# Last diagonal step of a group in full fp32 from summed operands, and a first block by two tiles

## The chip, the cores and the metric

The kernel runs on one core of a Trainium2 chip. The metric is the device time of that core in microseconds (us), read for the whole program. The engines are TensorE (PE in the profile, with its weight loads as PEld), VectorE (DVE), ScalarE (ACT), GpSimd (POOL) and SyncE (SP), which issues most of the DMAs.

## What is computed

An attention block and a channel mix on x of shape (2, 2048, 256), each with a layer norm without parameters in front and a residual behind. All matrices are 256x256 and fp32:

```
def attention(y):                       # y = layernorm(x)
    q = (y @ Wq + bq) / sqrt(256); k = y @ Wk + bk; v = y @ Wv + bv
    scores = where(causal, q k^T, -inf)         # 2048 x 2048 per batch
    return (softmax(scores) @ v) @ Wo + bo
def channel_mix(x):                     # x = layernorm(x)
    x_prev = x shifted by one row, first row 0
    xr = mu_r * x + (1 - mu_r) * x_prev;  xk = mu_k * x + (1 - mu_k) * x_prev
    return sigmoid(xr @ W_r.T) * (square(relu(xk @ W_k.T)) @ W_v.T)
x = x + attention(layernorm(x))
x = x + channel_mix(layernorm(x))
```

## The kernel before

**Numbers.** Most matmuls take operands rounded to fp32r. So that the result is near fp32, an operand is kept as a pair: ScalarE copies it out of PSUM as `_hi` in fp32r, VectorE or GpSimd subtracts that and leaves `_lo`. A product is then three matmuls, hi by hi, hi by lo and lo by hi (`product`, lines 794, 797 and 798). With 256 channels there are two chunks of 128 to contract (`KC` = 2), so one product is six matmuls. A few matmuls take plain fp32 operands without a split: the products of the weight matrices (lines 1002 and 1027).

**Tiles.** The 4096 rows are 32 tiles of 128. Four tiles make a group (512 queries), and the last of eight groups is treated in two halves. For each group the normalised rows are transposed (`xT`), multiplied by a folded matrix of Wq and Wk to give the keys (`kT`) and by a folded Wv and Wo to give the values (`v`). Then come steps of scores: step s takes 128 keys and all queries of the group that see them, so transposed scores of 128 x 512. The four steps on the diagonal see 512, 384, 256 and 128 queries. The last of them would have 128 columns. `scores` (lines 909 to 921) widens it to 256, so its six matmuls have 256 columns each, of which 128 are used. The causal mask is added by one bf16 matmul (line 796).

**After the scores.** ScalarE keeps a copy of the scores in a slot of `st` (16 slots of 512 columns), VectorE updates a running maximum (`take_max`), TensorE transposes the maximum (`mt`), VectorE reduces it, TensorE spreads it (`mb`), VectorE subtracts it (`shift`), ScalarE takes the exponential and rounds to `p_hi`, GpSimd makes `p_lo` (`weights_low`, line 364), and TensorE multiplies by the values (`pv`, lines 961 to 963, three matmuls per tile). The channel mix follows per group: transposes `hT`, products `kk`, `rr`, `ff`.

**Order.** Every engine runs one list, written by a loop over slots. In slot s stands score step s while there are any (79 of them), and the tables at lines 114 to 129 say in which slot each other stage stands (`PV_AT`, `XT_AT`, `KT_AT`, `V_AT`, `HT_AT`, `KK_AT`, `STATS_AT`, `APPLY_AT` and so on). All engines read the same tables, so a slot number sets the order on each engine, and semaphores do the rest. PSUM banks of TensorE's stages go round among three (`bank_w`), so a stage also waits until the stage three uses earlier has been read out (`free`).

**The start.** Ahead of the loop TensorE transposes the raw weights (line 969), multiplies Wk by Wq in plain fp32 into one bank (line 1002), transposes the first group (line 830), and makes its keys with twelve matmuls of 512 columns (line 1017). `idle` (line 986) runs matmuls on zeros in between, with counts from `IDLE`. ScalarE and VectorE take hi and lo of the folded matrix in one instruction each. On VectorE `ln1_apply` (line 595) writes the normalised rows, tile by tile, and a memset (line 599) closes a group.

Of the kernel before, what the change touches and what calls it, by code (L numbers as in the profile page):

```python
# [5 lines left out]
def attention_channel_mix_block(nc, y, wq, bq, wk, bk, wv, bv, wo, bo, w_r, w_k, w_v, mu_r, mu_k, out):  # L6
# [10 lines left out]
    B, T, C = y.shape  # L17
# [133 lines left out]
    LEAD = 2  # L151
    SLOTS = range(FIRST_SLOT, END)
# [34 lines left out]
    with ctx:  # L187
# [16 lines left out]
        peak = sb("peak", [P, 2, GW])  # L204
        peak_col = sb("peak_col", [P, 2, TG])
# [40 lines left out]
        early = (bank_o + bank_w[:NO - 1:-1])[:4]  # L246

# [3 lines left out]
        def bank_of(*use):  # L251
# [11 lines left out]
         last_mix_split, last_act_split, squared, single_squared, act_high, act_split, r_ready, gate_ready, ff_ready, ff_used, out_ready, last_out_ready) = [sem(n) for n in (  # L263
# [6 lines left out]
            "last_mix_split last_act_split squared single_squared act_high act_split r_ready gate_ready ff_ready ff_used out_ready last_out_ready").split()]  # L270
# [57 lines left out]
        def _(pool):  # L328
# [760 lines left out]
```

## Time and profile before

| | us |
|---|---|
| median of three runs | 365.44 (364.97 to 365.71) |
| the profiled execution | 365.21 |
| its span, first to last instruction | 363.2 |
| TensorE busy in the span | 353.2 (97%) |
| VectorE busy | 254.8 (70%) |
| ScalarE busy | 239.2 (66%) |
| GpSimd busy | 209.0 (58%) |

The span is what the trace covers; 2.0 us of the profiled execution lie around it. A matmul's record is longer than the distance to the next one, since matmuls are pipelined: what one costs is read from start to start. In a row of the timeline the first number is the start, the second the length of the piece, and xN the number of instructions that it merges.

### The profile page before, as it was taken

The numbers are of one execution on the slowest core, as the hardware profiler recorded it, in microseconds if no ns is written. First come the engines' busy times: TensorE is split into PE (matmuls) and PEld (weight loads), VectorE is DVE, ScalarE is ACT, GpSimd is POOL, SyncE is SP. The second block draws the span as 40 slices with busy tenths as digits, with TensorE's granted clock in tenths as the row PEclk, the third lists the DMA queues.
The fourth block names the chain that finished last, engine by engine and source line by source line (L and its number), as shares of the span: only waits on it lengthen the run. The fifth ranks groups of instructions, "written<-read, shape, count | busy, mean of one in ns | idle before, by whom it ended". The sixth has DMA issues, their size and how long they took to land.

```text
span 363.2 us, 6783 instructions
## 1 busy us (share of the span) xinstructions
PE 353.2 (97%) x2466; PEld 324.5 (89%) x2466; DVE 254.8 (70%) x569; ACT 239.2 (66%) x467; POOL 209.0 (58%) x246
## 2 busy tenths in 40 slices
PE   8999999999999999999999999999999999999995
PEld 6788888989899888899998989999999999989885
DVE  4597888698946786855568876786857558673645
ACT  2355543987659547597565679587368877789572
POOL 4013330468777743579644357678155768699781
PEclk9999999999999999999999999999999999999999
DMA  7600000000012003003000000030000000000001
GB/s 214 220 2 1 2 0 3 0 3 1 2 38 79 1 0 117 1 2 90 28 3 0 2 0 3 29 88 1 3 29 31 0 3 2 30 31 0 31 29 58
DMA packets 11905, 10.64 MB, mean 29 GB/s; under 512 B 1889, under 2 KB 11874, under 8 KB 11874
## 3 DMA queue, kind: packets, MB, share of 16 engines
q1 hardware_dynamic: 10512, 10.23, 8.8%
q8 instruction: 19, 0.31, 0.4%
q10 hardware_dynamic: 1362, 0.01, 0.2%
q14 instruction: 12, 0.10, 0.1%
HBM read 6.04 MB, written 4.19 MB: 28 GB/s over the span
## 4 chain that ended last, share of the span: by engine, by line
PE 76%; DVE 8%; POOL 6%; ACT 5%; issue 3%; DMA 1%; SPq 0%; ACTq 0%; DVEq 0%
PE W L794 16%; PE W L797 16%; PE W L798 15%; PE O L961 7%; PE O L963 7%; PE O L962 7%; PE W L830 3%; POOL kT_hi L364 3%; DVE mix L710 2%; DVE h_row L696 1%; POOL mix_lo L369 1%; DMA h_row<-in_L_attn_Wq_dram 1%; DVE st L675 1%; ACT mix L471 1%; ACT st L416 1%
## 5 line engine op out<-in xcount | busy, mean ns | idle before, releaser
L364 POOL TENSOR_TENSOR p_lo<-st,p_hi 128x512 fp32r<-128x512 f32 (+1 forms) x71 | 80.9, 1157 | 38.8 <-ACT p_hi L416 37.7
L663 DVE TENSOR_TENSOR peak<-peak,W 128x512 f32<-128x512 f32 (+3 forms) x70 | 42.2, 603 | 47.9 <-ACT st L416 47.7
L416 ACT ACTIVATE st<-W 128x512 f32<-128x512 f32 (+1 forms) x79 | 42.5, 538 | 42.3 <-PE W L798 42.2
L961 PE MATMUL O<-v_hi,p_hi 128*128 128x258 f32 x241 | 69.1, 287 | 0.2 <-DVE x_in L685 0.2
L963 PE MATMUL O<-v_hi,p_lo 128*128 128x258 f32 x241 | 68.0, 282 | 0.0
L962 PE MATMUL O<-v_lo,p_hi 128*128 128x256 f32 x241 | 67.7, 281 | 0.0
L797 PE MATMUL W<-xT_lo,kT_hi 128*128 128x512 f32 (+2 forms) x188 | 65.9, 350 | 0.0
L794 PE MATMUL W<-xT_hi,kT_hi 128*128 128x512 f32 (+2 forms) x188 | 64.4, 343 | 0.8 <-DVE kT_lo L573 0.8
L798 PE MATMUL W<-xT_hi,kT_lo 128*128 128x512 f32 (+2 forms) x188 | 63.2, 336 | 0.0
L452 ACT ACTIVATE st<-st 128x512 f32<-128x512 f32 (+1 forms) x79 | 44.8, 567 | 8.7 <-DVE st L675 8.6
L416 ACT ACTIVATE p_hi<-st 128x512 fp32r<-128x512 f32 (+1 forms) x71 | 40.4, 569 | 15.3 <-PE O L963 13.4
L369 POOL TENSOR_TENSOR mix_lo<-mix,mix_hi 128x512 fp32r<-128x512 f32 (+2 forms) x36 | 40.4, 1147 | 17.5 <-ACT mix_hi L416 17.5
L961 PEld LDWEIGHTS O<-v_hi,p_hi 128*128 128x128 f32 x241 | 45.4, 188 | 1.2 <-POOL p_lo L364 0.5
L962 PEld LDWEIGHTS O<-v_lo,p_hi 128*128 128x128 f32 x241 | 45.6, 189 | 0.3
L963 PEld LDWEIGHTS O<-v_hi,p_lo 128*128 128x128 f32 x241 | 45.5, 189 | 0.0
L675 DVE TENSOR_TENSOR st<-st,B 128x512 f32<-128x512 f32 (+1 forms) x79 | 43.2, 609 | 3.1 <-PE B L941 3.1
L794 PEld LDWEIGHTS W<-xT_hi,kT_hi 128*128 128x128 f32 x188 | 35.5, 189 | 3.6 <-DVE kT_lo L573 1.1
L798 PEld LDWEIGHTS W<-xT_hi,kT_lo 128*128 128x128 f32 x188 | 35.6, 190 | 3.3
L794 PE MATMUL W<-ffn_hi,mix_hi 128*128 128x256 f32 x128 | 37.0, 289 | 1.3 <-DVE mix_lo L573 0.7
L797 PEld LDWEIGHTS W<-xT_lo,kT_hi 128*128 128x128 f32 x188 | 35.9, 191 | 2.3
L797 PE MATMUL W<-ffn_lo,mix_hi 128*128 128x256 f32 x128 | 36.2, 282 | 0.0
L798 PE MATMUL W<-ffn_hi,mix_lo 128*128 128x256 f32 x128 | 36.1, 282 | 0.0
(138 smaller groups left out, 824.3 us busy)
## 6 DMA issues: line engine op xcount, KB each, us to landing
out_dram<-gate SPq DMA_DIRECT2D x15, 256.0 KB, 2.1
x_in<-in_L_attn_y_all_dram SPq DMA_DIRECT2D x7, 512.0 KB, 4.5
x_in<-in_L_attn_y_all_dram SPq DMA_DIRECT2D x2, 256.0 KB, 4.8
h_row<-in_L_attn_Wk_dram SPq DMA_DIRECT2D x1, 256.0 KB, 3.1
h_row<-in_L_attn_Wq_dram SPq DMA_DIRECT2D x1, 256.0 KB, 4.3
st<-in_L_attn_Wv_dram SPq DMA_DIRECT2D x1, 256.0 KB, 5.3
st<-in_L_attn_Wo_dram SPq DMA_DIRECT2D x1, 256.0 KB, 5.5
mix<-in_L_ffn_W_k_dram SPq DMA_DIRECT2D x1, 256.0 KB, 6.6
```

The costliest lines, as they stand in the source:

```text
L364: g.tensor_tensor(lo[:, r], score_tile(u), hi[:, r].bitcast(f32), ALU.subtract).then_inc(p_split, 1)
L369: g.tensor_tensor(mix_lo[:, j, r], mix[:, j, r], mix_hi[:, j, r].bitcast(f32), ALU.subtract).then_inc(mix_split, 1)
L416: a.activation(dst, src, ACT.Copy, **kw).then_inc(done, 1)
L452: a.activation(score_tile(u), score_tile(u), ACT.Exp).then_inc(exp_done, 1)
L663: v.tensor_tensor(peak[:, J % 2, r], peak[:, J % 2, r], scores, ALU.max).then_inc(maxed, 1)
L675: v.tensor_tensor(score_tile(u), score_tile(u), bank_b[:, cols_of(u)], ALU.subtract).then_inc(sub_done, 1)
L794: mm(dst, a_hi, b_hi, start=n == 0, stop=False)
L797: mm(dst, a_hi, b_lo, start=False, stop=False)
L798: last = mm(dst, a_lo, b_hi, start=False, stop=end)
L961: mm(o[:, 0:VW], hi[:, r], v_hi[:, j + b, :], start=j + b == 0, stop=False)
L962: mm(o[:, 0:C], hi[:, r], v_lo[:, j + b, :], start=False, stop=False)
L963: last = mm(o[:, 0:VW], lo[:, r], v_hi[:, j + b, :], start=False, stop=end)
```

## The change

Four things change.

1. The last diagonal step of each group of four tiles (seven of them) is no longer widened and split. GpSimd adds `_hi` and `_lo` again, into `own_x` (128 queries, two chunks, in the unused first half of an `st` slot) and `own_k` (128 keys), and TensorE multiplies these as plain fp32 with 128 columns: two matmuls and the mask instead of six and the mask. GpSimd does the two additions (128x256 each) in the slot before that step.
2. The first group is done by two tiles: the product of Wk and Wq goes chunk by chunk into two banks, the first transposes start once two tiles are normalised, and the keys are made with 24 matmuls of 256 columns instead of 12 of 512.
3. The counts of idle matmuls go from (6, 1, 5, 6, 1) to (6, 1, 3, 0, 0).
4. All tables of slots have new numbers.

```diff
-    XT_AT = {1: (2, 2), 2: (7, 9), 3: (23, 23), 4: (33, 34), 5: (43, 43), 6: (47, 50), 7: (61, 61)}
+    XT_AT = {1: (2, 2), 2: (8, 10), 3: (22, 23), 4: (31, 32), 5: (42, 42), 6: (48, 49), 7: (60, 60)}
...
-    FT_AT = [(-2,), (3,), (3,)]
-    IDLE = (6, 1, 5, 6, 1)
+    FT_AT = [(2,), (7,), (10,)]
+    IDLE = (6, 1, 3, 0, 0)
...
+    OWN_AT = [FIRST[J + 1] - 2 for J in range(NJ) if GROUPS[J][2] == TG]
...
+            def own(J):
+
+                G = GROUPS[J][0]
+                if J > 0:
+                    pool.wait_ge(s_ready, FIRST[J])
+                pool.wait_ge(xT_split, KC * (G + 1))
+                pool.wait_ge(kT_split, KC * (G + 1))
+                x, k = slice(GW - P, GW), slice(GW * (G % GB + 1) - P, GW * (G % GB + 1))
+                n = PLACES[FIRST[J + 1] - 2][0]
+                if n >= NR:
+                    pool.wait_ge(p_split, FILLED[n - NR] + 1)
+                g.tensor_tensor(own_x(J), xT_hi[:, G % NT, :, x].bitcast(f32), xT_lo[:, G % NT, :, x].bitcast(f32), ALU.add).then_inc(own_ready, 1)
+                g.tensor_tensor(own_k[:], kT_hi[:, :, k].bitcast(f32), kT_lo[:, :, k].bitcast(f32), ALU.add).then_inc(own_ready, 1)
...
             for s in SLOTS:
                 for u in P_IN[s]:
                     weights_low(u)
+                if s in OWN_AT:
+                    own(STEPS[s][0])
...
-            sc.wait_ge(fold_ready, 3)
-            high(wkq_hi[:], pairs(bank_b), fold_moved, scale=SCALE)
             for h in range(KC):
-                xT_part(0, h)
+                sc.wait_ge(fold_ready, 3 + h)
+                high(wkq_hi[:, h, :], folded[h][:, 0:C], fold_moved, scale=SCALE)
+            for i in range(2):
+                sc.wait_ge(xT_ready, i + 1)
+                high(xT_hi[:, 0, :, i * 2 * P:(i + 1) * 2 * P], pairs(bank_of("xT", 0, i)), xT_high)
...
-                if t == TG - 1:
-                    dve.wait_ge(xhat_done, TG * (G + 1))
-                    v.memset(xhat[:, :, 0:1], 1.0).then_inc(xhat_ready, 1)
+                if t == TG - 1 or G == 0 and t == 1:
+                    dve.wait_ge(xhat_done, TG * G + t + 1)
+                    v.memset(xhat[:, t - 1 if G == 0 else 0:t + 1, 0:1], 1.0).then_inc(xhat_ready, 1)
...
+                if n == TG and diagonal(s) == TG - 1:
+                    pe.wait_ge(own_ready, 2 * (J + 1))
+                    r = cols_of(s)
+                    mm(bank[:, r], own_k[:, 0, :], own_x(J)[:, 0, :], start=True, stop=False)
+                    mm(bank[:, r], ident_b[:], mask_b[:, P:], start=False, stop=False)
+                    mm(bank[:, r], own_k[:, 1, :], own_x(J)[:, 1, :], start=False, stop=True).then_inc(s_ready, 1)
+                    return
...
-            pe.wait_ge(q_taken, 1)
-            for h in range(KC):
-                for d in range(KC):
-                    last = mm(bank_b[:, h * C:(h + 1) * C], wkT[:, d, h * P:(h + 1) * P], wqT[:, d, :], start=d == 0, stop=d == KC - 1)
-            last.then_inc(fold_ready, 1)
+            for d in range(KC):
+                pe.wait_ge(q_taken, d + 1)
+                for h in range(KC):
+                    last = mm(folded[h][:, 0:C], wkT[:, d, h * P:(h + 1) * P], wqT[:, d, :], start=d == 0, stop=d == KC - 1)
+                    if d == KC - 1:
+                        last.then_inc(fold_ready, 1)
```

The instructions of TensorE at the start, from the product of the weight matrices (line 1002) to the first keys (line 1017), before:

```order
L1002 MATMUL B<-st 128x256 x4
L986 MATMUL O<-p_lo 128x512 x6
L830 MATMUL W<-ident,xhat 128x128 x8
L969 MATMUL O<-ident,st 128x128 x4
L986 MATMUL O<-p_lo 128x512
L1017 MATMUL W<-xT_hi,wkq_hi 128x512
```

And the same place now, where L1043 is that product, L866 the transposes of the first group and L1064 the keys:

```order
L1043 MATMUL B<-st 128x256 [waits q_taken,taken_ready,bias_ready]
L1043 MATMUL O<-st 128x256
L1043 MATMUL B<-st 128x256 [waits q_taken]
L1043 MATMUL O<-st 128x256
L866 MATMUL W<-ident,xhat 128x128 [waits xhat_ready]
L866 MATMUL W<-ident,xhat 128x128 x3
L1010 MATMUL O<-ident,st 128x128 [waits wv_loaded]
L1010 MATMUL O<-ident,st 128x128 x3
L866 MATMUL W<-ident,xhat 128x128 [waits xhat_ready]
L866 MATMUL W<-ident,xhat 128x128 x3
L1064 MATMUL W<-xT_hi,wkq_hi 128x256 [waits xT_high,fold_moved]
```

The seven idle matmuls are gone from here, the transposes stand in two halves with the transposes of Wv between them, and the keys start with 256 columns.

GpSimd's list behind the start, before; `rstd` is the factor of the layer norm for the next group:

```order
L394 COPY st<-cols 128x2 [waits col_loaded]
L349 TENSOR_SCALAR var_eps<-mean_var 128x4 [waits var1_ready]
L351 TENSOR_TENSOR rstd<-var_eps,minus_half 128x4 [waits eps1_ready]
L349 TENSOR_SCALAR var_eps<-mean_var 128x4 [waits var1_ready]
L351 TENSOR_TENSOR rstd<-var_eps,minus_half 128x4 [waits eps1_ready]
L364 TENSOR_TENSOR p_lo<-st,p_hi 128x512 [waits p_high]
```

And now:

```order
L417 COPY st<-cols 128x2 [waits col_loaded]
L358 TENSOR_SCALAR var_eps<-mean_var 128x4 [waits var1_ready]
L360 TENSOR_TENSOR rstd<-var_eps,minus_half 128x4 [waits eps1_ready]
L386 TENSOR_TENSOR st<-xT_hi,xT_lo 128x256 [waits kT_split,xT_split]
L387 TENSOR_TENSOR own_k<-kT_hi,kT_lo 128x256
L358 TENSOR_SCALAR var_eps<-mean_var 128x4 [waits var1_ready]
L360 TENSOR_TENSOR rstd<-var_eps,minus_half 128x4 [waits eps1_ready]
L373 TENSOR_TENSOR p_lo<-st,p_hi 128x512 [waits p_high]
```

The first pair of sums stands directly behind the factor of group 1. The other six pairs stand the same way in the slot before the last diagonal step of their group.

TensorE near the end, at the transposes `hT` of the last groups (L830 before), before; rows L961 to L963 are `pv`, rows L794 to L798 behind them the second half of `ff` of group 6:

```order
L963 MATMUL O<-v_hi,kT_hi 128x258
L830 MATMUL W<-ident,h_row 128x128 [waits h_ready,gate_ready]
L830 MATMUL W<-ident,h_row 128x128
L830 MATMUL W<-ident,h_row 128x128 [waits h_ready,gate_ready]
L830 MATMUL W<-ident,h_row 128x128
L830 MATMUL W<-ident,h_row 128x128 [waits h_ready,ff_used]
L794 MATMUL W<-ffn_hi,mix_hi 128x256 [waits act_split,mu_done]
L797 MATMUL W<-ffn_lo,mix_hi 128x256
```

And now, where L858 is the transpose and L1002 to L1004 are `pv`:

```order
L1004 MATMUL O<-v_hi,kT_hi 128x258
L858 MATMUL W<-ident,h_row 128x128 [waits h_ready,gate_ready]
L858 MATMUL W<-ident,h_row 128x128
L858 MATMUL W<-ident,h_row 128x128 [waits h_ready,ff_used]
L858 MATMUL W<-ident,h_row 128x128
L1002 MATMUL O<-v_hi,kT_lo 128x258 [waits p_split]
L1003 MATMUL O<-v_lo,kT_lo 128x256
L1004 MATMUL O<-v_hi,kT_hi 128x258
```

The third transpose, which waits for `ff_used`, no longer follows the other two: thirteen tile products of `pv` (39 matmuls) stand between, and both halves of `ff` stand ahead of all of them.

## Rows read from the trace of the kernel before

**Rows 1.** The page: busy time by engine, and the chain that ended last.
```profile
PE 353.2 (97%) x2466; PEld 324.5 (89%) x2466; DVE 254.8 (70%) x569; ACT 239.2 (66%) x467; POOL 209.0 (58%) x246
...
PE 76%; DVE 8%; POOL 6%; ACT 5%; issue 3%; DMA 1%; SPq 0%; ACTq 0%; DVEq 0%
```

**Rows 2.** Timeline of TensorE, a masked score step with 256 columns, then group 1's transposes.
```profile
23.60 0.28 PE L794 MATMUL W<-xT_hi,kT_hi 128*128 128x256 f32 x1
23.72 0.23 PE L796 MATMUL W<-mask_b,ident_b 128*128 128x128 bf16 x1
23.76 0.36 PE L797 MATMUL W<-xT_lo,kT_hi 128*128 128x256 f32 x1
23.96 0.28 PE L798 MATMUL W<-xT_hi,kT_lo 128*128 128x256 f32 x1
...
24.32 0.28 PE L798 MATMUL W<-xT_hi,kT_lo 128*128 128x256 f32 x1
24.94 1.16 PE L830 MATMUL W<-ident,xhat 128*128 128x128 f32 x8 [0.34 <-DVE xhat L599]
```

**Rows 3.** Timeline of TensorE at the start: plain fp32 product, idle matmuls, transposes.
```profile
1.44 2.93 PE L986 MATMUL O<-p_lo 128*128 128x512 f32 x6 [1.44 <-DVE p_lo L629]
...
7.46 1.97 PE L1002 MATMUL B<-st 128*128 128x256 f32 x8
9.08 1.75 PE L986 MATMUL O<-p_lo 128*128 128x512 f32 x6
10.67 1.03 PE L830 MATMUL W<-ident,xhat 128*128 128x128 f32 x8
11.54 0.60 PE L969 MATMUL O<-ident,st 128*128 128x128 f32 x4
```

**Rows 4.** Timeline of TensorE: first keys, fold of Wv and Wo, first scores.
```profile
12.22 0.40 PE L1017 MATMUL W<-xT_hi,wkq_hi 128*128 128x512 f32 x1
...
14.97 1.03 PE L1027 MATMUL O<-st 128*128 128x256 f32 x4
...
17.52 0.60 PE L979 MATMUL W<-ident,mix 128*128 128x128 f32 x4
17.88 0.48 PE L794 MATMUL W<-xT_hi,kT_hi 128*128 128x512 f32 x1
```

**Rows 5.** Timeline of ScalarE at the start.
```profile
6.48 0.84 ACT L532 ACTIVATE st<-O,minus_first 128x255 f32<-128x255 f32 x2
```

**Rows 6.** Timeline of VectorE at the start, its rows for xhat among them.
```profile
8.60 0.73 DVE L595 TENSOR_SCALAR xhat<-x_in,mean_var,rstd 128x256 f32<-128x256 f32 x2 [0.26 <-POOL rstd L351]
9.62 0.74 DVE L595 TENSOR_SCALAR xhat<-x_in,mean_var,rstd 128x256 f32<-128x256 f32 x2 [0.29 <-POOL rstd L351]
...
18.35 0.69 DVE L573 TENSOR_TENSOR wvo_lo<-O,wvo_hi 128x512 fp32r<-128x512 f32 x1 [1.49 <-ACT wvo_hi L416]
...
22.81 0.56 DVE L663 TENSOR_TENSOR peak<-peak,W 128x384 f32<-128x384 f32 x1 [0.19 <-ACT st L416]
23.28 1.38 DVE L595 TENSOR_SCALAR xhat<-x_in,mean_var,rstd 128x256 f32<-128x256 f32 x4
```

**Rows 7.** Timeline of GpSimd at the start.
```profile
21.86 1.04 POOL L351 TENSOR_TENSOR rstd<-var_eps,minus_half 128x4 f32<-128x4 f32 x1
```

**Rows 8.** Groups of instructions by form: GpSimd's subtractions (line, form, xcount, busy, mean ns).
```profile
L364 POOL TENSOR_TENSOR p_lo<-st,p_hi 128x512 fp32r<-128x512 f32 x50 | 64.7, 1309 | 30.9 <-ACT p_hi L416 29.9
L364 POOL TENSOR_TENSOR p_lo<-st,p_hi 128x256 fp32r<-128x256 f32 x7 | 5.6, 805 | 0.0
```

**Rows 9.** VectorE's instructions on the tile h_row: ns min/median/max.
```profile
L696 DVE TENSOR_SCALAR h_row<-x_in,mean_var,per_tile x32: 406/412/1462, 43.1 to 351.1; 128x256 f32<-128x256 f32 x32
```

**Rows 10.** Timeline of VectorE, then of GpSimd, around 94.3 us.
```profile
94.24 0.76 DVE L696 TENSOR_SCALAR h_row<-x_in,mean_var,per_tile 128x256 f32<-128x256 f32 x1
...
93.56 1.29 POOL L378 TENSOR_TENSOR mix_lo<-mix,mix_hi 128x512 fp32r<-128x512 f32 x1
```

**Rows 11.** Waits of TensorE: what for, us in total, times, longest.
```profile
PE B L932 <- DVE peak L663: 0.9, 1, 0.9
PE W L794 <- DVE kT_lo L573: 0.8, 1, 0.8
PE W L794 <- DVE mix_lo L573: 0.7, 1, 0.7
PE W L830 <- DVE gate L742: 0.7, 1, 0.7
...
PE W L794 <- DVE gate L742: 0.3, 1, 0.3
PE O L961 <- DVE x_in L685: 0.2, 1, 0.2
```

More of the change, by code:

```diff
@@ L131, in stages @@
+    END = 674
+    FT_AT = [(2,), (7,), (10,)]
+    IDLE = (6, 1, 3, 0, 0)
     def stages(s):
@@ L204, in attention_channel_mix_block @@
         peak = sb("peak", [P, 2, GW])
+        own_k = sb("own_k", [P, KC, P])
         peak_col = sb("peak_col", [P, 2, TG])
@@ L246, in attention_channel_mix_block @@
         early = (bank_o + bank_w[:NO - 1:-1])[:4]
+        folded = (bank_b, early[0])
         def o_of(G, p):
@@ L831, in transposes, with first_xT @@
                 return last
+            def first_xT(i):
+                pe.wait_ge(xhat_ready, i + 1)
+                for h in range(KC):
+                    for t in range(2):
+                        last = nc.tensor.transpose(bank_of("xT", 0, i)[:, (2 * h + t) * P:(2 * h + t + 1) * P], xhat[:, 2 * i + t, h * P:(h + 1) * P], ident[:])
+                last.then_inc(xT_ready, 1)
             def xT(G, h):
                 free("xT", G, h)
-                pe.wait_ge(xhat_ready, G + 1)
+                pe.wait_ge(xhat_ready, G + 2)
                 transposes(bank_of("xT", G, h), xhat, h, range(TG)).then_inc(xT_ready, 1)
@@ L1004, in _ @@
             idle(IDLE[3])
-            for h in range(KC):
-                xT(0, h)
+            first_xT(0)
             pe.wait_ge(wv_loaded, 16)
             transposed(raw_v, early[2])
+            first_xT(1)
             idle(IDLE[4])
             xh, xl = xT_hi[:, 0], xT_lo[:, 0]
-            pe.wait_ge(fold_moved, 1)
-            for w, x, done in ((wkq_hi, xh, xT_high), (wkq_lo, xh, fold_split), (wkq_hi, xl, xT_split)):
-                for k in range(KC):
-                    pe.wait_ge(done, 1 if done is fold_split else k + 1)
-                    for h in range(KC):
-                        last = mm(bank_of("kT", 0, h)[:], w[:, k, h * P:(h + 1) * P], x[:, k, :], start=x is xh and w is wkq_hi and k == 0,
-                                  stop=x is xl and k == KC - 1)
-                        if x is xl and k == KC - 1:
-                            last.then_inc(kT_ready, 1)
+            for i in range(2):
+                c = slice(i * 2 * P, (i + 1) * 2 * P)
+                for w, x, done in ((wkq_hi, xh, xT_high), (wkq_lo, xh, fold_split), (wkq_hi, xl, xT_split)):
+                    for k in range(KC):
+                        if done is fold_split:
+                            pe.wait_ge(done, k + 1)
+                        else:
+                            pe.wait_ge(fold_moved, k + 1)
+                            pe.wait_ge(done, i + 1)
+                        for h in range(KC):
+                            last = mm(bank_of("kT", 0, h)[:, c], w[:, k, h * P:(h + 1) * P], x[:, k, c], start=x is xh and w is wkq_hi and k == 0,
+                                      stop=x is xl and k == KC - 1)
+                            if x is xl and i == 1 and k == KC - 1:
+                                last.then_inc(kT_ready, 1)
```

57 lines of the change are left out of this document (29 added, 28 removed).

## The prediction

> **What bounds the kernel now.** I read the page's busy times first, then the chain that ended last, then TensorE's waits, and last its timeline from start to start. TensorE is busy 97% of the span and is 76% of the chain; GpSimd, the engine that gets new work, is busy 58% [rows 1]. TensorE's waits are few and short: the longest behind the start are 0.9, 0.8, 0.7 and 0.7 us, once each [rows 11]. So the kernel is a row of matmuls issued without a break, and a matmul taken out anywhere gives back its own pitch (start to start), unless it stood just ahead of a wait. What the other engines do counts only where it makes one of those waits longer or shorter. The profiled execution took 365.21 us, 2.0 more than its span of 363.2; the median of the runs is 365.44. I sum against 365.21 and add 0.2 at the end.
>
> **Part 1, the last diagonal step.** Before, it is six matmuls of 256 columns and a mask. The step shown has the same form: it starts at 23.60, its last matmul at 24.32, and a pitch is 0.12, so it ends at 24.44 and costs 0.84 us [rows 2]. The mask's share is 0.12: 0.04 to the next start, and 0.20 instead of 0.12 behind that. Now there are two plain fp32 matmuls of 128 columns and the same mask. The trace has no such matmul, but it has two neighbours. A plain fp32 matmul of 256 columns appears as two records: four of them are the 8 records from 7.46 to 9.08, 0.20 us each. A plain fp32 transpose of 128 columns is one record: 8 of them from 10.67 to 11.54, 0.109 each [rows 3]. Lower bound: half the columns, half the time, 0.10 a record. Upper bound: no shrinking at all, 0.20. I take 0.11, from the row that has 128 columns and the same weight load. Four records and the mask: 4 x 0.11 + 0.12 = 0.56. Saved: 0.28 a step, 7 steps, **1.9 us** (2.2 at the lower bound; at the upper 4 x 0.20 + 0.12 = 0.92, a loss of 0.6).
>
> What it adds is on GpSimd: two sums of 128x256 a group, 14 in all. The nearest row is a subtraction of that form, 0.8 us [rows 8]: 1.6 us a group, 11 us over the span, on an engine with 154 us free. It is hidden if the pair is done when TensorE reaches the step. I went through the seven places. Groups 1, 3, 5 and 6 have little on GpSimd there. In group 2 (slot 22) the pair stands behind the `p_lo` of step 10, which waits for an earlier `pv`: after that `pv` come the exponential's copy and `p_lo` (about 1.6 us) and the pair (1.6), against 4.1 us of TensorE work (a score step 0.84, half an `xT` 0.44, half a `v` 1.4, a `pv` 1.4). In group 4 (slot 42) ten `pv` follow, and the next `p_lo` behind the pair cannot start before the first of them is done anyway. So I cost it at nothing there. If that cover went, it would cost up to 1.6 us a group.
>
> **Part 2, the start.** Before: the product at 7.46, first transposes at 10.67, keys at 12.22, fold of Wv and Wo at 14.97 [rows 3, 4]. Now: the two activations that the product waits for run from 6.48 to 7.32 [rows 5], and the product may start on the first, at about 6.95, to end at about 8.7. Two tiles are normalised at 9.33 [rows 6], so the first half of the transposes runs from 9.45 to 9.9, Wv's to 10.35, and the second half waits for tile four at 10.36 and the memset: 10.5 to 10.95. The keys: 24 x 0.118 = 2.85 us from 10.95, to 13.8, if hi and lo keep up. VectorE's lo of the folded matrix stands behind the last tile, at 10.5 to 11.2, its first lo of `xT` at 11.8, and TensorE asks for that one at 11.9. So 13.85 against 14.97: **1.1 us** earlier, and the first scores 1.1 us earlier too, once the transposes of an FFN matrix (0.36, 17.52 to 17.88 [rows 4]), now in slot 2, are set aside.
>
> Then comes the place that decides what remains: group 1's transposes, which already waited for VectorE at 24.94, 0.5 us later than the pitch would have it [rows 2]. VectorE has one instruction fewer ahead (a lo of an FFN matrix), so its statistics end about 1.7 us earlier, and GpSimd's factor, ready at 22.90 before [rows 7], comes at about 21.2. But `xhat` of group 1 also stands behind two running maxima, which follow the scores: 23.28 before [rows 6], about 21.9 now, and four instructions of it take 1.38. Undisturbed it ends at 23.3, TensorE arrives at 22.95, and the wait shrinks to 0.4. It is not undisturbed: GpSimd's first pair of sums stands right behind that factor, from about 21.2 to 22.8. What happens to VectorE then is in the trace. `h_row` is the same kind of instruction as `xhat`, a tensor by scalars from SBUF to SBUF, and takes 0.41 us in the median and up to 1.46 [rows 9]; the one at 94.24 took 0.76, beside a GpSimd subtraction that ran until 94.85 [rows 10]. It stands still until GpSimd's instruction is through. So I expect `xhat` to end at about 24.2 and the transposes to start at 24.3 instead of 24.94. Set against that, 0.36 us of transposes still has to be done behind it. What is left of the 1.1 us is **0.3**. Bounds: 0.2 with all of the pair in the way, 1.25 with none.
>
> The Trainium skill has this as a rule (SBUF — State Buffer, Who interferes with whom): VectorE in its two-port mode and GpSimd take a shared pair of ports for a whole instruction, and the other fully blocks. The trace agrees, as the 1.46 us against 0.41 shows. By a view in which the two engines don't meet, the start would give the 1.25.
>
> **Part 3, idle matmuls.** Nine of 19 go. They filled waits and nothing waits for them: two ahead of the product and six ahead of the transposes stood where TensorE waits for ScalarE and VectorE anyway, as counted above. So they count nothing.
>
> **Part 4, the tables.** They move no work in or out, so they can only change waits. Behind the start the waits of [rows 11] are, at a pitch of 0.12, somewhat dearer from start to start than the view says. (a) The wait for `kT_lo`, 0.8 (0.9 from start to start): the lo of group 3's keys stood on VectorE behind four residual chains; it now stands a slot earlier, ahead of two of them, and two score-sized stages follow before its bank is asked for. Gone. (b) The wait of a transpose for `gate`, 0.7 (0.9): now 39 matmuls of `pv` stand between. Gone. (c) The wait of `v` for `gate`, 0.3 (0.4): the bank now comes from an `rr`, which ScalarE reads out at once, instead of an `ff`. Gone. (d) The wait of `pv` for `x_in`, 0.2 (0.3): 5.6 us of FFN products stand between now. Gone. (e) The wait for `peak`, 0.9: group 2's last step is still followed at once by the transpose of the maximum, with more work on VectorE ahead. It stays. (f) The wait for `mix_lo`, 0.7, is in the tail behind the last `pv`, whose order is the same. It stays. That is 2.5 us. A new order of 305 stages makes waits of its own, and I set 0.7 us for them, the size of one of the long ones: **1.8 us**.
>
> **Sum.** 1.9 + 0.3 + 1.8 = 4.0 us. 365.21 - 4.0 = 361.2, and by the median **361.4**.
>
> **Rivals.**
>
> A. No collision at the start: the sums run while VectorE is busy on PSUM operands, or VectorE gets in first. For it: the pair may start earlier than I think, and be half done. Against it: `xhat` and the sums wait for the same factor. 1.25 instead of 0.3: 360.4.
>
> B. The waits move but don't shrink: the four that go come back elsewhere, where VectorE is at 70% and gets delayed by GpSimd's new sums. Parts 1 and 2 remain: 2.2 us, 363.2.
>
> C. Plain fp32 records don't get shorter with 128 columns. Part 1 then loses 0.6 instead of gaining 1.9: 363.9. Against it: the transposes at 0.109.
>
> D. TensorE's clock. All rows have the granted clock at full, yet the first six idle matmuls of 512 columns took 2.72 us, 0.45 each [rows 3], against 0.23 later. With nine fewer and gaps of up to 0.8 us, the keys' 24 matmuls could run at half speed: 2.8 us more, 364.2.
>
> E, the slower side. GpSimd's pair is late and TensorE waits at every one of the seven steps. The place: pairs behind a `p_lo` and a lo of the mix, at 1.3 us each [rows 8]. With both ahead, 2.6 + 1.6 us stand against some 3.2 us of TensorE work in a slot or two, 1.0 us late, 7.0 in all: 4.0 - 7.0, so 368.4. It decides from 0.6 us a step. Against it: ahead of these subtractions GpSimd mostly idles for ScalarE, 29.9 us in all [rows 8], which is no backlog, and I found such a queue in one group at most.
>
> **Chances.** Forecast 0.50, A 0.17, B 0.15, C 0.05, D 0.05, E 0.08. This measurement tells apart about 0.2%, 0.7 us. Below 364.7 lie the forecast, A, nearly all of B, and most of C and D: faster 0.86. Within: 0.06, from the edges of B, C and D. Slower: 0.08, E. The range 359.6 to 364.5 holds A to most of D and leaves out E and the far edges; the forecast's own range is 360.4 to 362.4.
>
> **What would show it.** Part 1: four records at a pitch near 0.11 in the last diagonal step, and no wait of TensorE for `st` or `own_k`. A pitch of 0.20 is C, such waits are E. Part 2: keys from 10.95 to 13.85, then group 1's transposes at about 24.3, with `xhat` instructions above 0.41 us beside GpSimd's sums; at 23.4 it is A. Part 4: no wait for `kT_lo` near 130 us and none for `gate`, and waits behind the start that sum to 1.8 us less. What would make the forecast wrong above all is a wait I haven't seen in the middle of the span, where TensorE has no slack to win it back.

## The result

The changed kernel takes 363.82 us (median of 4 runs, 363.47 to 364.01) against 365.56 (4 runs, 364.97 to 365.71). The ratio is 0.9954, 95% interval 0.9937 to 0.9972. That is 1.74 us or 0.46% faster. The direction was as forecast, the size less than half of the forecast's 4.0 us (361.4). The time lies inside the range (359.6 to 364.5) and outside the likeliest case's own (360.4 to 362.4). The profiled execution took 363.47, with a span of 361.5. In the runs further down, one execution of the kernel before and one of the last variant took 495 and 489 us at a granted clock of 0.66, and are left out of the ratios.

### The profile page after: what moved, and what is told of

It reads as the page before. It is cut to its first block, busy times and chain, and to the rows that moved or that the text cites. A ratio compares the mean times of both kernels' runs of the same rounds, so it can differ in the third digit from the quotient of the medians.

```text
span 361.5 us, 6804 instructions
## 1 busy us (share of the span) xinstructions
PE 351.0 (97%) x2455; PEld 322.1 (89%) x2455; DVE 256.4 (71%) x571; ACT 239.2 (66%) x468; POOL 220.7 (61%) x260
## 4 chain that ended last, share of the span: by engine, by line
PE 85%; POOL 6%; DVE 5%; ACT 2%; issue 1%; ACTq 0%; DVEq 0%
PE W L822 17%; PE W L825 17%; PE W L826 17%; PE O L1002 8%; PE O L1004 8%; PE O L1003 8%; PE W L858 3%; POOL kT_hi L373 2%; POOL mix_lo L392 2%; PE B L982 1%; PE B L973 1%; POOL mix_lo L401 1%; PE O L1027 1%; DVE xhat L621 1%; DVE xT_lo L599 1%
## 5 line engine op out<-in xcount | busy, mean ns | idle before, releaser
L1002 PE MATMUL O<-v_hi,p_hi 128*128 128x258 f32 x241 | 69.1, 287 | 0.0
L1004 PE MATMUL O<-v_hi,p_lo 128*128 128x258 f32 x241 | 68.0, 282 | 0.0
L822 PE MATMUL W<-xT_hi,kT_hi 128*128 128x512 f32 (+2 forms) x174 | 61.2, 352 | 0.2 <-DVE xT_lo L599 0.2
L825 PE MATMUL W<-xT_lo,kT_hi 128*128 128x512 f32 (+2 forms) x174 | 61.4, 353 | 0.0
L826 PE MATMUL W<-xT_hi,kT_lo 128*128 128x512 f32 (+2 forms) x174 | 59.3, 341 | 0.0
L392 POOL TENSOR_TENSOR mix_lo<-mix,mix_hi 128x512 fp32r<-128x512 f32 (+2 forms) x36 | 41.8, 1186 | 14.0 <-ACT mix_hi L441 14.0
L1002 PEld LDWEIGHTS O<-v_hi,p_hi 128*128 128x128 f32 x241 | 45.4, 189 | 0.7 <-POOL p_lo L373 0.3
L1004 PEld LDWEIGHTS O<-v_hi,p_lo 128*128 128x128 f32 x241 | 45.5, 189 | 0.0
L826 PEld LDWEIGHTS W<-xT_hi,kT_lo 128*128 128x128 f32 x174 | 32.9, 189 | 3.4
L822 PEld LDWEIGHTS W<-xT_hi,kT_hi 128*128 128x128 f32 x174 | 32.8, 189 | 3.3 <-DVE xT_lo L599 0.6
L825 PEld LDWEIGHTS W<-xT_lo,kT_hi 128*128 128x128 f32 x174 | 33.2, 191 | 2.2
```

What stands on the lines that cost most here:

```text
L822: mm(dst, a_hi, b_hi, start=n == 0, stop=False)
L825: mm(dst, a_hi, b_lo, start=False, stop=False)
L826: last = mm(dst, a_lo, b_hi, start=False, stop=end)
L1002: mm(o[:, 0:VW], hi[:, r], v_hi[:, j + b, :], start=j + b == 0, stop=False)
L1004: last = mm(o[:, 0:VW], lo[:, r], v_hi[:, j + b, :], start=False, stop=end)
```

## The profile after

The page, as [rows 1]: TensorE has 2.2 us less to do, GpSimd 11.7 more.

```profile
PE 351.0 (97%) x2455; PEld 322.1 (89%) x2455; DVE 256.4 (71%) x571; ACT 239.2 (66%) x468; POOL 220.7 (61%) x260
...
PE 85%; POOL 6%; DVE 5%; ACT 2%; issue 1%; ACTq 0%; DVEq 0%
```

TensorE's waits, as [rows 11] (what for: total, times, longest):

```profile
PE B L973 <- DVE peak L691: 1.8, 1, 1.8
PE O L1027 <- DVE p_lo L655: 1.4, 1, 1.4
PE W L858 <- DVE xhat L625: 0.9, 1, 0.9
PE W L822 <- DVE mix_lo L599: 0.7, 1, 0.7
PE W L822 <- ACT mix L496: 0.5, 2, 0.3
PE W L858 <- DVE h_row L724: 0.5, 1, 0.5
PE W L946 <- DVE xT_lo L599: 0.4, 1, 0.4
PE B L982 <- DVE peak_col L696: 0.3, 1, 0.3
```

The four waits that were to go, for `kT_lo`, twice for `gate`, and for `x_in`, are gone. In their place the wait for `peak` has doubled from 0.9, `xhat` went from 0.3 to 0.9, `h_row` from 0.3 to 0.5 and `peak_col` from 0.2 to 0.3, and the one for `xT_lo` is new. The wait for `mix` is 0.5 in all, as before, in two pieces.

TensorE at a last diagonal step (start, us, engine, operation), as [rows 2]:

```profile
47.74 0.38 PE L946 MATMUL W<-st,own_k 128*128 128x128 f32 x2
47.95 0.22 PE L947 MATMUL W<-mask_b,ident_b 128*128 128x128 bf16 x1
48.01 0.44 PE L948 MATMUL W<-st,own_k 128*128 128x128 f32 x2
48.21 0.48 PE L822 MATMUL W<-xT_hi,kT_hi 128*128 128x512 f32 x1
48.52 0.39 PE L825 MATMUL W<-xT_lo,kT_hi 128*128 128x512 f32 x1
```

Two records take 0.21, the mask 0.06, two more 0.20, and the next row's pitch is 0.31 instead of 0.23: 0.55 us a step, where 0.56 was forecast.

TensorE at the start, as [rows 3, 4], then group 1's transposes and its last step:

```profile
7.63 0.67 PE L1043 MATMUL B<-st 128*128 128x256 f32 x2
...
13.99 1.02 PE L1074 MATMUL O<-st 128*128 128x256 f32 x4
...
24.12 1.16 PE L858 MATMUL W<-ident,xhat 128*128 128x128 f32 x8 [0.93 <-DVE xhat L625]
...
26.16 0.49 PE L946 MATMUL W<-st,own_k 128*128 128x128 f32 x2 [0.44 <-DVE xT_lo L599]
```

The product starts at 7.63 and not at 6.95, since the two activations ahead of it came 0.54 us later than in [rows 5] (7.02 for 6.48); the transposes behind it wait for the normalised tiles in any case, so the keys end at 13.99 (forecast 13.85). Group 1's transposes start at 24.12 (forecast 24.3). VectorE and GpSimd ahead of these transposes, as [rows 6, 7]:

```profile
22.02 1.82 DVE L621 TENSOR_SCALAR xhat<-x_in,mean_var,rstd 128x256 f32<-128x256 f32 x4
```
```profile
21.29 0.74 POOL L386 TENSOR_TENSOR st<-xT_hi,xT_lo 128x256 f32<-128x256 f32 x1
21.98 0.74 POOL L387 TENSOR_TENSOR own_k<-kT_hi,kT_lo 128x256 f32<-128x256 f32 x1
```

Four `xhat` take 1.82 instead of 1.38: the collision that was forecast, at half its size. The forecast had all four stand still until the pair is through, and end at 24.2. Only the first was held up, 0.85 us instead of 0.41, and they ended at 23.84. The wait that grew most is that for `peak`. VectorE ahead of it, before:

```profile
73.98 4.15 DVE L710 SCALAR_TENSOR_TENSOR mix<-hT,cols,mix 128x512 f32<-128x512 f32 x4
78.16 0.58 DVE L717 COPY hT<-hT 128x2 f32<-128x2 f32 x1
78.65 0.28 DVE L663 TENSOR_TENSOR peak<-peak,W 128x128 f32<-128x128 f32 x1
```

And now VectorE, then GpSimd, then TensorE:

```profile
75.53 2.10 DVE L738 SCALAR_TENSOR_TENSOR mix<-hT,cols,mix 128x512 f32<-128x512 f32 x2
77.67 1.12 DVE L745 COPY hT<-hT 128x2 f32<-128x2 f32 x1
78.70 0.68 DVE L599 TENSOR_TENSOR xT_lo<-W,xT_hi 128x512 fp32r<-128x512 f32 x1
79.30 0.68 DVE L599 TENSOR_TENSOR v_lo<-W,v_hi 128x512 fp32r<-128x512 f32 x1
79.90 0.27 DVE L691 TENSOR_TENSOR peak<-peak,W 128x128 f32<-128x128 f32 x1
```
```profile
77.04 2.95 POOL L392 TENSOR_TENSOR mix_lo<-mix,mix_hi 128x512 fp32r<-128x512 f32 x2
```
```profile
78.10 0.44 PE L948 MATMUL W<-st,own_k 128*128 128x128 f32 x2
80.31 0.63 PE L973 MATMUL B<-ident,peak 128*128 128x128 f32 x4 [1.78 <-DVE peak L691]
```

The new order puts `xT_lo` and `v_lo` (0.6 us each from start to start) ahead of the last running maximum, and a copy of one column of `hT` takes 1.12 us beside GpSimd's `mix_lo`. VectorE's row between the last two maxima is not longer for it: two `mix` fewer stand there, and it takes 4.7 us where it took 5.0. What shrank more is TensorE's work beside it. The end of the score step before is at 74.58 now and was at 72.47. From there TensorE reaches the transpose of the maximum in 3.7 us (it took 5.5), because half a `v`, half an `xT`, four tile products of `pv` and the shorter step stand there instead of twelve tile products, half an `hT` and the longer step. The maximum lets it go on after 5.7 us (it took 6.6). The difference is the wait, 2.0 us instead of 1.1 from the end of one step to the next start. At 80.31 TensorE resumes: whatever had been gained before that point and was not also gained on VectorE is lost there.

## The experiments

Each time is the median of 4 to 12 runs. The kernel before, in the same calls, had medians of 365.28 to 365.56. TensorE's wait of 1.4 for `p_lo`, ahead of 7 us, is in every kernel and left out.

### The parts, one by one and in pairs

**The fp32 step alone** (tables, start and `IDLE` of before):

```
+ own_ready, own_k, own_x, own(J) in slot FIRST[J + 1] - 2, the branch in scores
  PV_AT, MT_AT, ... IDLE as before
```

> The kernel before with the last diagonal step in plain fp32 and GpSimd's pairs of sums, its tables and start untouched. Theory (the trace after shows 0.56 us a step, 0.84 before): seven steps give 1.9 us, if the pairs delay nothing: 363.6. Rival (the pairs slow VectorE through the shared port where TensorE waits for VectorE, as at the wait for peak, 0.8 us, and at group 1's xhat, 0.4 us): it gives only 0.7 to 1.0 us: 364.6.

Measured: 370.23, ratio 1.0142 (1.0126 to 1.0159), slower by 5.0 us. Both cases missed. TensorE's longest wait, then GpSimd ahead of it:

```profile
PE W L936 <- POOL own_k L386: 3.3, 3, 1.6
```
```profile
48.17 0.24 POOL L357 TENSOR_SCALAR per_tile<-mean_var 128x1 f32<-128x1 f32 x1 [4.46 <-DVE mean_var L713]
...
49.04 0.72 POOL L385 TENSOR_TENSOR st<-xT_hi,xT_lo 128x256 f32<-128x256 f32 x1
49.72 0.77 POOL L386 TENSOR_TENSOR own_k<-kT_hi,kT_lo 128x256 f32<-128x256 f32 x1
```

This is the forecast's rival E, in the old order and at three of seven steps. At 48 us GpSimd has no backlog. It sits for 4.46 us behind a factor that waits for VectorE, and the pair is queued behind that. Idle time on GpSimd was no proof that it would be on time. The waits for `own_k` are 3.3 of the 6.9 us between the 1.9 gained and the 5.0 lost. Most of the rest is in other waits that grew: `peak` from 0.9 to 2.0, `xhat` from 0.3 to 0.8, `xT_lo` to 0.4, and a new one of 0.5 for `p_lo`.

**The start alone** (old tables, new `IDLE`):

```
  first_xT, keys by halves, hi and lo of the fold by chunks; IDLE = (6, 1, 3, 0, 0)
  scores, own, PV_AT ... as before
```

> The kernel before with the start by two tiles and idle counts (6, 1, 3, 0, 0), old tables, old last step. Theory: keys end 1.0 us earlier and, since no pair of sums stands behind group 1's factor, group 1's transposes too: 0.9 to 1.1 us faster, 364.5. Rival (the start is bound by VectorE's chain to xhat of group 1 whatever comes before): at most 0.4 us faster.

Measured: 363.41, ratio 0.9946 (0.9933 to 0.9959), 1.9 us faster, so faster than the whole change. Group 1's transposes start at 23.93 instead of 24.94: 1.0 us. The other 0.9 is the wait for `kT_lo`, which no line of this edit touches. VectorE and GpSimd in this kernel, then in the kernel before:

```profile
124.85 0.73 DVE L700 TENSOR_SCALAR h_row<-x_in,mean_var,per_tile 128x256 f32<-128x256 f32 x2
```
```profile
125.39 2.60 POOL L379 TENSOR_TENSOR mix_lo<-mix,mix_hi 128x512 fp32r<-128x512 f32 x2
```
```profile
126.05 1.77 DVE L696 TENSOR_SCALAR h_row<-x_in,mean_var,per_tile 128x256 f32<-128x256 f32 x2
```
```profile
126.37 2.60 POOL L378 TENSOR_TENSOR mix_lo<-mix,mix_hi 128x512 fp32r<-128x512 f32 x2
```

VectorE moved by 1.2 us and GpSimd by 1.0. That is enough for the pair of `h_row` to be nearly done when `mix_lo` begins (0.73 us), instead of being caught by it (1.77). `kT_lo` comes behind, in time.

**Step and start, old tables:**

> The change with the tables of before. Theory (the new tables gave waits back as fast as they took them away, and stretched two): within 0.4 us of the changed kernel or faster than it, 363.4 to 364.0; TensorE keeps the old waits for kT_lo and gate and has none longer than 1.2 us. Rival (the tables carry the gain, as the prediction had it at 1.8 us): 365.3 or more.

Measured: 367.94, ratio 1.0071 (1.0059 to 1.0083), with 3.4 us of waits for `own_k`. The new tables are worth 4.1 us on top of it, mostly because in them the pairs are on time.

**Start and tables, with the old last step:**

> The changed kernel with the old last step: six matmuls of 256 columns, no pairs of sums. Theory: 1.9 us of matmuls come back and about 1.2 us of waits go (peak of group 2 from 1.8 to about 1.0, xhat of group 1 from 0.9 to 0.5), so it is 0.5 to 1.0 us slower than the changed kernel: 364.5. Rival (the pairs cost nothing): 1.9 us slower, 365.7, and the wait for peak stays 1.8 us.

Measured: 365.67, ratio 1.0021 (1.0007 to 1.0034). So in the new order the fp32 step is worth 1.85 us, pairs included, as the sum had it. Beside the start alone the new tables cost 2.3 us. (Five of its twelve spans are 1.6 us longer than the other seven; by those seven, 363.2, the step is worth 1.7 and the tables cost 1.9. Their granted clock is 0.995 over the span, against 0.998 to 1.000 in the other seven. No trace of a long one was kept; what such a span is in another kernel is shown below.) The wait for `peak` is 1.9 here, with no pair on GpSimd, and those for `xT_lo` are 0.8: in the new order they are there without the pairs.

### Where the pairs stand

**The step alone in the old order, pairs issued some slots ahead:**

```
- OWN_AT = [FIRST[J + 1] - 2 ...]
+ OWN_SLOT = {0: -3, 1: 7, 2: 20, 3: 36, 4: 41, 5: 47, 6: 58}
```

> The run own_only, which was 5 us slower than before, with GpSimd's pairs of sums one to four slots earlier in its list (group 0 ahead of the loop, group 1 slot 7, group 2 slot 20, group 3 slot 36, group 4 slot 41, group 5 slot 47, group 6 slot 58); nothing else. Theory (TensorE lost the time to pairs that stood behind work that waits for VectorE, 3.3 us in three waits for own_k, and to their collisions with VectorE at xhat and peak): the three waits go, the wait for xhat falls from 0.8 to 0.4, and it is 4 to 5 us faster than own_only: 365.5 or less. Rival (GpSimd has no room for 11 us of sums wherever they stand): 368 or more.

Measured: 364.63, ratio 0.9985 (0.9976 to 0.9994). No wait for `own_k` is left, and 5.6 us are back against the same kernel with late pairs. 0.8 us remain of the 1.9 that the step saves. The rest goes into waits on VectorE and GpSimd, which TensorE now reaches sooner: `peak` from 0.9 to 1.3, `xT_lo` from 0.1 to 0.4, and a new one of 0.3 for `p_lo`.

**The changed kernel with group 1's pair ahead of the loop:**

```
+ OWN_SLOT.update({0: -3})
```

> The changed kernel with the first pair of sums ahead of the loop, so that it stands in front of the factor of group 1 instead of behind it. Theory (the pair holds up xhat of group 1): the four xhat instructions take 1.4 us instead of 1.8, the transposes of group 1 start 0.4 us earlier, and it is 0.3 to 0.5 us faster: 363.4. Rival (something else than the pair stretches them): they still take 1.8 us and the time is the same.

Measured: 363.17, ratio 0.9943 (0.9930 to 0.9956), 0.65 us faster than the change. The longest `xhat` is 413 ns instead of 851.

**The start and the early pairs together, in the old order:** the dictionary of slots above, with the two-tile start.

> Kernel before with the two-tile start, the last step in fp32 and the pairs of sums issued early (group 1 ahead of the loop, the others at slots 7 to 58, several slots ahead of their step), all in the OLD order. Theory (the order is what turns the parts into gains, and a pair that stands early enough costs nothing): what the start alone gave (1.9 us) and what the early pairs gave on the old order (0.8) add up: 362.2 to 363.0, no wait for own_k, no wait for kT_lo, so below the whole change (363.82) with no new tables. Rival (every shift of the work makes waits of its own, and the two don't add): 363.4 or more, with new waits of 0.5 us or longer.

Measured: 362.63, ratio 0.9927 (0.9915 to 0.9939). The two gains, 1.9 and 0.8, add up to the measured 2.7. With none of the new tables the kernel is 1.2 us faster than the change.

### Three tries to move a wait

> The changed kernel with the second half of group 0's mix two slots later (slot 24 instead of 22), so that VectorE's maximum of step 23 no longer stands behind two mix instructions and the copy of hT. Theory (the wait for peak of 1.8 us is VectorE's list, stretched by GpSimd's subtractions): that wait falls to at most 0.9 us and the time by about 1.0: 362.8. Rival (the wait is the latency from the last step through ScalarE and VectorE, whatever stands ahead): it stays above 1.5 us.

The edit is `MIX_AT[0]` from (21, 22) to (21, 24). Measured: 375.03, ratio 1.0255 (1.0240 to 1.0269), a clear miss. The wait for `peak` did fall to 0.8, but another came:

```profile
PE W L822 <- POOL mix_lo L392: 8.8, 2, 8.6
```

In its new slot GpSimd's `mix_lo` stands behind three `p_lo` and three factors that wait for VectorE. The last of these ended at 98.3, the `mix_lo` at 100.7, and TensorE waits 8.6 us for it with all its later work. From 96 to 102 us the granted clock was 0.52. So this run says nothing on whether the maximum alone would have gained.

> The changed kernel with the transposes of group 2's maximum behind step 24 instead of right behind step 23 (mt and mb of group 2 in slot 24). Theory: 1.9 us of TensorE work (half an xT, half a v) and a step of 1.4 us now cover the wait for peak, so it goes, and nothing behind it is late: 1.5 to 2.0 us faster, 362.1. Rival (the softmax of group 3 then comes too late, and pv waits for p_lo instead): less than 0.5 us faster, with a new wait of pv.

The edit is `MT_AT[2]` and `MB_AT[2]` from 23 to 24, so `xT` and `v` come ahead of the maximum. Measured: 364.42, ratio 0.9970 (0.9959 to 0.9982), 0.6 slower than the change. The wait for `peak` is gone, and TensorE waits for whatever comes next from VectorE:

```profile
PE W L858 <- DVE xT_lo L599: 0.9, 1, 0.9
...
PE W L822 <- DVE xT_lo L599: 0.8, 2, 0.5
```

> The changed kernel with group 1's pair ahead of the loop, and its last pv issued at slot 203 instead of 208, ahead of the products kk of group 8 and the mix of its first half. Theory (the tail gave back 0.6 us because GpSimd's 1/std of the last tile stands behind four subtractions and h_row, the last transposes and the last mix follow it): that 1/std comes about 1.5 us earlier, TensorE's waits for h_row (0.5) and one of those for mix go: 0.4 to 1.0 us faster than with the pair alone (363.17), 362.2 to 362.8. Rival (the tail is bound by the row of products between, or the 1/std now holds up mix_lo): within 0.2 us of 363.2, or slower.

The edit, beside the early pair, is the last entry of `PV_AT` from 208 to 203. Measured: 364.99, ratio 0.9993 (0.9984 to 1.0002), 1.8 slower than the kernel it was made from. The rival's mechanism, GpSimd then TensorE:

```profile
347.41 0.57 POOL L361 TENSOR_TENSOR per_tile<-per_tile,minus_half 128x1 f32<-128x1 f32 x1
347.95 0.91 POOL L393 TENSOR_TENSOR mix_lo<-mix,mix_hi 128x128 fp32r<-128x128 f32 x2
```
```profile
349.01 0.36 PE L823 MATMUL W<-mix_hi,ffn_hi 128*128 128x256 f32 x1 [1.80 <-POOL mix_lo L393]
```

The factor came 1.1 us earlier (347.41 against 348.54), and now the `mix_lo` that TensorE needs is late. Behind this wait the granted clock was 0.57 from 350 to 354 us. That is in a profiled execution with a span of 362.9; four of the eleven, with spans of 362.4 and 362.5 and a clock of 0.998 or more, are still 1.4 us slower than the kernel it was made from.

### What a long wait costs besides

**The changed kernel without GpSimd's sums:**

```
- mm(bank[:, r], own_k[:, 0, :], own_x(J)[:, 0, :], ...)
+ mm(bank[:, r], kT_hi[:, 0, k].bitcast(f32), xT_hi[:, G % NT, 0, x].bitcast(f32), ...)
- if s in OWN_AT: own(STEPS[s][0])
```

> The changed kernel without GpSimd's sums: the last step multiplies the hi parts alone in fp32, so it leaves out the lo parts of 128 keys and queries a group and what they add to the scores. Same four records, no wait for own_k. Theory (in the new order the sums still cost through the port they share with VectorE and through the queue): 0.7 to 1.4 us faster than the changed kernel, 362.4 to 363.1; xhat of group 1 loses its 0.5 us, the wait for peak stays at 1.7 or more because the order makes it. Rival (the sums are hidden, as the forecast has it): 363.6 to 364.0. Second rival (the sums make the wait for peak as well): below 362.2, with that wait at 1.0 or less.

Measured: 364.77, ratio 0.9972 (0.9958 to 0.9985), with less work and 0.95 us slower than the change. None of the three cases. The ten spans fall in two heaps: four at 361.3 to 361.5, as in the changed kernel (361.5), and six at 362.7 to 363.1. A window of the profiled execution, which is of the second heap (length, busy of PE, PEld, DVE, ACT, POOL, granted clock, DMA), and one matmul and the next in it:

```profile
78.00:84.00 6.00, 3.88 (x23) 3.83 (x23) 4.49 (x10) 2.09 (x5) 3.56 (x6) 0.77 0.01 3
```
```profile
81.02 0.42 PE L820 MATMUL W<-wvo_hi,xT_hi 128*128 128x256 f32 x1
81.23 0.42 PE L823 MATMUL W<-wvo_lo,xT_hi 128*128 128x256 f32 x1
```

The wait for `peak` is 2.1 here, and behind it TensorE runs at its lower level, 1.2 GHz: a 256-column matmul has a pitch of 0.21 us instead of 0.12.

**The same with the wait filled:**

```
  gather_peak(J), behind pe.wait_ge(sub_done, FIRST[J]):
+ if J == 2: keep_warm(6)      # six matmuls 128x512, result unused
```

> The kernel without GpSimd's sums (its last step multiplies the hi parts alone), and in TensorE's wait for the running maximum of group 2, near 78.3 us, six matmuls of 128x512 whose result nothing uses (6 x 0.23 = 1.4 us, inside a wait of 2.1). Theory (without them the granted clock goes to the half level behind that wait, in six of ten executions, and the 256-column matmuls then take 0.213 instead of 0.118 for some 4 us, 1.5 us in all): now the clock stays at 1.00 there in all executions, spans near 361.4 alone, median 363.5 against 364.77. Rival (the two spans have another cause): both spans appear again, median between 363.5 and 364.8, some executions at 362.9 or more.

Measured: 363.53, ratio 0.9951 (0.9937 to 0.9965), five spans of 361.2 to 361.7, and the clock at 1.00:

```profile
78.00:84.00 6.00, 5.34 (x37) 4.56 (x36) 5.21 (x12) 2.53 (x6) 3.57 (x6) 1.00 0.00 0
```

So the clock drop is shown, and it costs 1.5 us where it happens. Without it, a kernel that needs no sums is level with the change. In the one without the sums group 1's transposes come 0.5 us earlier (23.65), but TensorE gets `peak` at 80.20 against 80.31, because `mix_lo` then collides for longer with VectorE's `mix` (3.35 us for two instead of 2.95, and `mix` 2.45 instead of 2.10).

### Taking the stalled copy out of VectorE's row

```
  DVE mix_part, j == 3:  + if J == n: pass        (no tensor_copy)
  ACT mix_part, j == 3:  + if J == n: a.activation(hT[:, :, 0:1], hT[:, :, GW:GW + 1], ACT.Copy).then_inc(prev_ready, 1)
```

> The changed kernel with group 1's pair ahead of the loop, and the copy of one column of hT behind the mix of group 2 made by ScalarE instead of VectorE. On VectorE it takes 1.1 us, beside GpSimd's mix_lo, where 0.17 us are enough, and it stands ahead of the maximum that TensorE waits for (1.8). Theory (the stall of VectorE beside GpSimd makes that much of the wait): the wait for peak falls to 0.7 to 1.0, the median by 0.7 to 1.1, 362.1 to 362.5. Rival (what follows on VectorE keeps TensorE waiting there, as when the maximum was transposed later): gain below 0.3, 362.9 or more, with a new wait between 80 and 90 us.

> The old order with the two-tile start and the pairs of sums issued early (362.63), with the same copy made by ScalarE. VectorE's copy takes 0.58 us there, and TensorE's wait for peak is 1.3. Theory: 0.3 to 0.5 us faster, 362.1 to 362.3, with the wait for peak at 0.8 to 1.0. Rival (the gain goes into the next wait on VectorE): 362.5 or more.

These two had n = 2: 363.16 (ratio 0.9940, 0.9927 to 0.9953) and 362.63 (0.9923, 0.9910 to 0.9936), the times they had before. They test nothing of the theory: the copy at 77 us is that of group 0, and it still stood there. The next two have n = 0.

> As the kernel with group 1's pair ahead of the loop (363.17), but the column of hT behind the mix of group 0, the instruction that stands at 77.13 us on VectorE for 1.12 us ahead of the maximum that TensorE waits for, is copied by ScalarE. Theory (VectorE's stall beside GpSimd makes that much of the wait): the wait for peak falls from 1.8 to 0.7 to 1.0, the median by 0.5 to 1.1, 362.1 to 362.7. Rival (VectorE's row keeps TensorE waiting whatever is taken out, as when the maximum was transposed later): gain below 0.3, 362.9 or more, with a new or longer wait between 80 and 90 us.

Measured: 362.26, ratio 0.9922 (0.9908 to 0.9935), 0.91 us faster than the kernel it was made from. The wait, and VectorE ahead of it:

```profile
PE B L978 <- DVE peak L694: 0.8, 1, 0.8
```
```profile
75.08 2.10 DVE L741 SCALAR_TENSOR_TENSOR mix<-hT,cols,mix 128x512 f32<-128x512 f32 x2
77.22 0.69 DVE L602 TENSOR_TENSOR xT_lo<-W,xT_hi 128x512 fp32r<-128x512 f32 x1
```

> The old order with the two-tile start and the pairs of sums issued early (362.63), and the same copy of group 0 made by ScalarE; on VectorE it takes 0.58 us there, and TensorE's wait for peak is 1.3. Theory: 0.3 to 0.5 us faster, 362.1 to 362.3, wait for peak 0.8 to 1.0. Rival (the gain goes into the next wait on VectorE): 362.5 or more.

Measured: 362.18, ratio 0.9914 (0.9900 to 0.9928), 0.45 faster than with the copy on VectorE; the wait for `peak` went from 1.3 to 0.9. Both gains stayed to the end. This is the fastest kernel of the study: 1.6 us under the change, 3.2 under the kernel before, in the old order.

## Why the prediction was right or wrong

**Part 1 (1.9 us): right.** 0.55 us a step was measured for 0.56, and 1.7 to 1.85 us for the seven, from the changed kernel with and without it. "I cost it at nothing" holds for the pairs only in the new order: in the old one they cost 6.9 (1.9 + 5.0). The argument given, no backlog and enough work of TensorE in between, was not what made it right. What counts is the wait at which GpSimd's list stands.

**Part 2 (0.3 us): right in mechanism and near in size.** The keys ended 0.14 us later than forecast, though the product started 0.7 later, and group 1's transposes started 0.2 us earlier, since the stall of `xhat` was half of what was forecast. Against [rows 2] they start 0.82 earlier, of which the postponed transposes of an FFN matrix take back 0.36. Behind them the own step waits 0.44 for its bank, and these FFN transposes now stand between it and `xT`; that wait was not in the sum. It is 0.4 with the old last step in the new order too, and was 0.1, at these transposes, in the kernel before. Moving the pair gave 0.65 us, so rival A's 1.25 was there in part, for another slot number.

**Part 3 (nothing): held as far as seen.** The first keys had the full clock, so rival D did not come at the start. It came elsewhere, in variants with a wait of 1.8 us or more ahead of it.

**Part 4 (1.8 us): the step that failed.** Its first half was right: the four waits went, 2.0 us in the view and the forecast's 2.5 from start to start. The other half, "0.7 us for waits of its own" and "(e) stays", was mis-sized. In the view of waits `peak` grew by 0.9 and `h_row` by 0.2, two for `xT_lo` (0.4 and 0.2) and two of 0.2 for GpSimd's `mix_lo` and `p_lo` are new: 2.1 us, and some 2.9 from start to start, since each wait also costs TensorE its overlap (that for `peak` 1.8 in the view, and 2.0 from the end of the step at 78.3 to 80.3). The prediction saw "more work on VectorE ahead" of the maximum and gave it no price. It looked at one engine only. The two lo's there cost 1.2 us from start to start and the copy of a column 1.0, but two `mix` went, and VectorE's row got 0.3 shorter. TensorE's work beside it got 1.8 shorter, and that was not set against it. The net of the tables is therefore not a gain: beside the start they cost 1.9 to 2.3 us. Of the 2.5 us, 0.9 were not theirs: the wait for `kT_lo` goes with the start alone. The changed kernel's 1.7 is then 1.9 + 0.4 + 2.5 - 2.9, within 0.2.

**Additivity failed too.** The sum took the parts as independent. Measured in us against before: start -1.9, step +5.0, start and step +2.7, start and tables +0.4, all three -1.7. The tables are the price of the step's pairs in their slots, and the early pairs get 0.8 us of the step's 1.9 without them.

**The tail (f)** kept its wait of 0.7 for `mix_lo`, but gave back 0.6 us. The last `pv` ended 2.1 us earlier than before, and the last transposes of `h_row` started 1.5 earlier, since GpSimd made the last tile's factor behind subtractions. GpSimd there, then VectorE:

```profile
347.13 0.88 POOL L392 TENSOR_TENSOR mix_lo<-mix,mix_hi 128x128 fp32r<-128x128 f32 x2
348.00 0.73 POOL L401 TENSOR_TENSOR mix_lo<-mix,mix_hi 128x256 fp32r<-128x256 f32 x1
348.71 0.22 POOL L358 TENSOR_SCALAR per_tile<-mean_var 128x1 f32<-128x1 f32 x1
```
```profile
349.61 0.54 DVE L724 TENSOR_SCALAR h_row<-x_in,mean_var,per_tile 128x256 f32<-128x256 f32 x1 [1.65 <-POOL per_tile L360]
```

Of the rivals B was nearest, at 363.2, by its mechanism too: the waits came back elsewhere on VectorE. C is excluded by the pitch of 0.1. E is real, but only in the old order, and at three of seven steps.

What stays open: which of the new tables' many entries carries the loss, apart from those around 78 us, and why the clock falls behind the same wait in some executions and not in others.

## What to carry to other kernels

Where one engine runs without a break, a shift of another engine's list is not free. Price each instruction that newly stands between a producer and the consumer that waits, set it against the work that the consumer still has in that stretch, and look for the next wait that the other engine sets, since all that is gained ahead of it can end there. Place small helper work some slots early, judged by what its engine's list waits for and not by how idle the engine is, and test each part alone before a new order hides what it costs.

## What the runs showed of the hardware

- **A tiny instruction can stall longest.** The copy of one column of `hT` on VectorE takes 0.17 us at least, in the median 1.13 in the changed kernel (six of them), and 0.37 before. On ScalarE the one of group 0 took 0.19:

```profile
L745 DVE COPY hT<-hT x6: 169/1130/1155, 77.7 to 316.2; 128x2 f32<-128x2 f32 x6
```
```profile
L519 ACT ACTIVATE hT<-hT 128x2 f32<-128x2 f32 x1 | 0.2, 193 | 0.0
```

  The Trainium skill (SBUF — State Buffer, Who interferes with whom) has GpSimd and VectorE, in its two-port mode, take a shared pair of ports for a whole instruction, and the other wait. The stalls agree: five of the six copies end 0.03 us behind a GpSimd subtraction, and the sixth, with none beside it, took the 0.17.
- **The stall goes both ways.** GpSimd's sum of 128x256 takes 0.74 us and, beside VectorE's `mix`, up to 1.20.
- **Plain fp32 with 128 columns** costs 0.10 to 0.11 us a record, two records to a matmul.
- **The granted clock can fall within a full program.** Behind a wait of 2.1 us it did in six of ten executions, at a cost of 1.5 us; behind 1.8 us at 80 us in none of the four of the changed kernel. Six matmuls of 128x512 in the wait of 2.1 kept it at 0.997 or more over the span in five executions of five.
